# Chunk attention's loop: the order of scores and output product on TensorE, and of maxima and moments on VectorE

## The reference

```python
Q = (x @ Wq + bq).reshape(b, nc, CHUNK, e)      # CHUNK = 64, nc = 16, e = 256
K = (x @ Wk + bk).reshape(b, nc, CHUNK, e)
V = (x @ Wv + bv).reshape(b, nc, CHUNK, e)
local_scores = jnp.einsum('bnqe,bnke->bnqk', Q, K) * scale
local = jnp.einsum('bnqk,bnke->bnqe', jax.nn.softmax(local_scores, axis=-1), V)
cross_scores = jnp.einsum('bnqe,bmke->bnmqk', Q, K) * scale
cross = jnp.einsum('bnmqk,bnke->bnqe', jax.nn.softmax(cross_scores, axis=-1), V)
out = (local + cross).reshape(b, s, e) @ Wo + bo
x = _layernorm(x + out, axis=-1)
```

## Time and profile before

| | |
|---|---|
| median of 3 runs | 1342.64 us (1342.58 to 1343.19) |
| profiled execution | 1344.01 us |
| its span | 1342.3 us |
| TensorE matmul, weight load busy | 1173.1 us, 872.3 us |
| VectorE, ScalarE, GpSimd busy | 846.0, 789.7, 609.5 us |
| mean granted TensorE clock | 0.941 |

### The profile page before, as it was taken

How to read it: one execution, slowest core, us unless ns; L and a number is a source line. 1 busy time by engine, 2 the same in 40 slices (tenths; PEclk the granted TensorE clock), 3 DMA queues, 4 the chain that set the end, 5 groups by cost and what they waited for, 6 DMA issues and landing times. The chain is left out here.

```text
span 1342.3 us, 25832 instructions
## 1 busy us (share of the span) xinstructions
PE 1173.1 (87%) x8247; PEld 872.3 (65%) x8248; DVE 846.0 (63%) x1511; ACT 789.7 (59%) x2121; POOL 609.5 (45%) x641
## 2 busy tenths in 40 slices
PE   7888489667799999999989999999899856999991
PEld 4554267455566777777666677777577645888881
DVE  2588789884245555656345556666577658888883
ACT  2488347424556555665555556655367767777773
POOL 1277537647454521431363322310056614888873
PEclk9999779897699999999999999999999857999996
DMA  9100000000110000000100000100190041333334
GB/s 300 49 1 0 0 1 2 1 16 16 29 36 17 17 17 17 17 17 2 32 16 19 15 18 17 48 1 1 30 347 2 1 167 53 55 55 51 55 51 138
DMA packets 42266, 58.03 MB, mean 43 GB/s; under 512 B 6992, under 2 KB 34768, under 8 KB 42160
## 3 DMA queue, kind: packets, MB, share of 16 engines
q1 hardware_dynamic: 34672, 46.44, 11.5%
q0 software_dynamic: 7488, 10.23, 4.7%
HBM read 32.54 MB, written 13.63 MB: 34 GB/s over the span
## 5 line engine op out<-in xcount | busy, mean ns | idle before, releaser
L2100 DVE TENSOR_REDUCE ga_neg_top<-ps 128x1 f32<-128x128 f32 (+7 forms) x256 | 182.1, 753 | 193.8 <-PE ps L1870 193.5
L1990 ACT COPY ga_e_tr<-ps 128x512 f32<-128x512 f32 (+3 forms) x192 | 92.0, 479 | 173.8 <-PE ps L1879 170.9
L1981 ACT ACTIVATE ga_e<-ps,ga_neg_top 128x128 f32<-128x128 f32 (+7 forms) x256 | 188.2, 743 | 7.5 <-DVE ga_neg_top L2100 6.8
L1879 PE MATMUL ps<-ident,ga_e 128*128 128x128 f32 x1152 | 165.2, 278 | 0.9 <-DVE ga_e_tr L2108 0.8
L1895 PE MATMUL ps<-ga_e_tr,ga_v 128*64 128x256 f32 x1152 | 151.7, 391 | 4.1 <-ACT ga_att L1998 4.1
L1879 PEld LDWEIGHTS ps<-ident,ga_e 128*128 128x128 f32 x1152 | 123.3, 142 | 28.1 <-ACT ga_e L1981 14.7
L2108 DVE COPY ga_e_tr<-ps 128x128 f32<-128x128 f32 (+3 forms) x192 | 106.0, 552 | 35.0 <-PE ps L1879 34.7
L2651 DVE TENSOR_TENSOR ex_w_lo<-ex_gate_up,ex_w_hi 128x1024 fp32r<-128x1024 f32 x78 | 95.5, 1225 | 34.0 <-ACT ex_w_hi L2522 32.0
L2055 POOL TENSOR_TENSOR ga_q_lo<-shared,ga_q_hi 128x1024 fp32r<-128x1024 f32 x15 | 35.5, 2368 | 174.9 <-ACT ga_q_hi L1971 174.9
L1895 PEld LDWEIGHTS ps<-ga_e_tr,ga_v 128*64 128x64 f32 x1152 | 72.5, 136 | 48.9 <-issue 23.3
L489 ACT ACTIVATE ca_e<-ps,ca_neg_top 128x64 f32<-128x64 f32 x256 | 76.7, 358 | 36.2 <-DVE ca_neg_top L528 36.2
(11 more groups left out here) (334 smaller groups left out, 2801.3 us busy)
## 6 DMA issues: line engine op xcount, KB each, us to landing
shared<-shared SPq DMA_DIRECT2D x80, 128.0 KB, 2.4
ex_gate_up<-in_ex_gate_up SPq DMA_DIRECT2D x1, 8192.0 KB, 24.4
ex_down<-in_ex_down SPq DMA_DIRECT2D x1, 4096.0 KB, 35.7
x_tr<-in_x_tr SPq DMA_DIRECT2D x4, 512.0 KB, 6.7
x_nat<-in_x SPq DMA_DIRECT2D x1, 2048.0 KB, 11.6
gated_rows<-shared SPq DMA_DIRECT2D x4, 512.0 KB, 4.5
x_tr<-summed_rows SPq DMA_DIRECT2D x8, 256.0 KB, 4.0
out<-x_tr SPq DMA_DIRECT2D x8, 256.0 KB, 2.1
```

What stands on the lines that cost most here:

```text
L1879: last = nc.tensor.transpose(ps_tr[n % 2][:, (kb - k0) * P:(kb - k0 + 1) * P], e[half][t % 2][:, kb * P:(kb + 1) * P], core.ident[:])
L1981: nc.scalar.activation(e[half][t % 2][:, 0:blocks(t) * P], ps_scores(t, half), ACT.Exp, bias=neg_top[t % 2][:, half:half + 1], accum_out=s ...
L1990: nc.scalar.copy(e_tr[g % 2][:, k0:k1, half, t % 2 * P:(t % 2 + 1) * P], ps_tr[n % 2][:, 0:(k1 - k0) * P].rearrange("p (k t) -> p k t", t= ...
L2100: nc.vector.tensor_reduce(neg_top[t % 2][:, half:half + 1], ps_scores(t, half), AX.X, ALU.max, negate=True).then_inc(top_ready, 1)
```

## The change

On TensorE, the matmul y of u5 with its two waits moves from ahead of the scores of u1 to behind them. On VectorE, z and the moments of u5 (four instructions) move from ahead of the maxima of u1 to behind neg_top. No instruction is added or removed, and no buffer or semaphore changes.

```diff
@@ TensorE, step(...) @@
                         last.then_inc(q_ready, 1)
-                    if u5 is not None:
-                        pe.wait_ge(diag_tr_copied, u5 + 1)
-                        tail.pe_output_free(pe, u5)
-                        nc.tensor.matmul(tail.y, diag_tr[:], vw[:, u5, :], start=True, stop=True).then_inc(tail.y_ready, 1)
                     if u1 is not None:
                         ps = ps_scores[(turn - 1) % 2]
                         pe.wait_ge(q_copied, u1 + 1)
...
                         last.then_inc(s_ready, 1)
+                    if u5 is not None:
+                        pe.wait_ge(diag_tr_copied, u5 + 1)
+                        tail.pe_output_free(pe, u5)
+                        nc.tensor.matmul(tail.y, diag_tr[:], vw[:, u5, :], start=True, stop=True).then_inc(tail.y_ready, 1)
                     if at(u2, TILES - 1):
                         following.pe_context(pe)
@@ VectorE, step(...) @@
                                                 bq[:].unsqueeze(2).to_broadcast([P, KD, P]), ALU.add).then_inc(q_copied, 1)
-                    if u5 is not None:
-                        tail.dve_variance(dve, u5)
                     if u1 is not None:
                         link = Chain(dve, first_step, u1, 1)
                         dve.wait_ge(s_ready, u1 + 1)
...
                         nc.vector.tensor_scalar_mul(neg_top[(turn - 1) % 2][:], top[:], -SCALE).then_inc(top_ready, 1)
                         link.end()
+                    if u5 is not None:
+                        tail.dve_variance(dve, u5)
                     if u4 is not None:
```

## The result

The changed kernel takes 1344.84 us (median of 20 runs, of which one, of 2859.01 us, is left out of the ratio), the kernel before 1342.39 us in as many; the ratio is 1.0016, 95% interval 1.0008 to 1.0023. On 1342.4 us that is +2.1 us, between +1.1 and +3.1. The forecast was +1.0 us; the time lies inside its range, and the sign and the mechanism came as forecast, but the sum was too small by about half. The same kernel measured again gave 1.0010 (1.0000 to 1.0021), +1.3 us, so how far the forecast was too small isn't sharp.

What follows compares the result with a forecast made beforehand. The prediction took two loops of waits, through TensorE and GpSimd, to bound the turn. Entry +0.8, three turns 0 and eight turns +0.2 gave +1.0 us: 1343.6 us by the median, range 1341.0 to 1346.0.

Steps and rivals of the forecast that it cites:

- The bound: Old loop turn of 6.11 us: TensorE's loop through diag_tr and y takes 6.07, GpSimd's through probs and halves 5.95.
- neg_top is held: VectorE's neg_top, due at 2.03 us after xn's start, is held 0.8 us by GpSimd's probs on shared SBUF ports.
- The turn of 6.13: New loop turn, summed along VectorE from xn to the next xn with neg_top held: 6.13 us in place of 6.11.
- The entry, +0.8: Turn from 66.78 us: z0 and its variance come behind neg_top 4, so the block sum is 0.8 us late.
- Eight turns, +0.2: Last eight of the twelve turns: 6.13 us each in place of 6.11, together +0.2 us.
- A shorter wait gives none back: TensorE's granted clock is 1.00 in all these turns, so shortening its wait gains nothing through the clock.
- TensorE runs ahead until it needs only xn and q: In the new turn, y waits for the previous turn's copy, so TensorE's scores are ready when the maxima are due.
- The drain only shifts: After the last scores the old and new orders are the same, so the drain moves in time without changing.
- That neg_top isn't held: Rival: neg_top unheld in its new place, GpSimd's loop of 5.95 us sets the turn; 1341.6 us, chance 0.15.
- That it loses the race between probs and halves: Rival: halves takes the ports before neg_top, which ends 1.34 us later in every turn; 1358 us, chance 0.10.
- That TensorE's wait was the whole bound: Rival: neither hold nor GpSimd's loop counts, VectorE's chain sets turns near 5.6 us; 1338 us, chance 0.05.
- That diag is held too: Rival: VectorE's diag is also held and a second hold follows, 0.3 us a turn; 1347 us, chance 0.05.

Runs made afterwards that it cites:

- VectorE's half alone: Kernel before with only VectorE's part of the edit, y still ahead of the scores on TensorE: 1369.07 us, ratio 1.0191.
- The two runs with probs early: Changed kernel and kernel before, each with maxima in PSUM, recip ahead of the block sum, GpSimd's store behind halves: 1346.84 us (1.0029) and 1347.89 us (1.0040).
- their repair: The two runs with probs early, with probs now also waiting for xn: new order 1339.33 us (0.9990), old order 1340.76 us (0.9989).
- the maxima in PSUM alone: Only the 16 maxima moved from SBUF to PSUM: changed kernel 1343.61 us (1.0011), kernel before 1340.09 us (0.9989).
- TensorE's half alone: Kernel before with only TensorE's part of the edit, y behind the scores, VectorE's order as before: 1343.97 us, ratio 1.0010.
- the first profile: First profile of the changed kernel, which measured 1344.84 us (1.0016); its twelve turns took 75.81 us.
- the second: Second profile, from the unaltered changed kernel measured again: 1343.26 us, ratio 1.0010; its twelve turns took 74.26 us.
- the third profile: Changed kernel unaltered, profiled again for the clock alone; twelve turns 74.24 us, first drain turn 7.74 us.
- the run with the filler: Changed kernel with 16 additional TensorE transposes of a constant into an idle bank in the last turn ahead of the loop: 1343.92 us, ratio 1.0007.
- new order from the loop on: Changed kernel with the old order kept in the written-out turns 0 to 7, the new one only from the loop on: 1342.25 us, ratio 1.0007.

## Why the prediction was right, and where it was too small

**The bound (right).** Two loops of nearly equal length, TensorE's and GpSimd's. VectorE's half alone makes the first longer, and the turns follow it to 7.2 and more. The two runs with probs early and their repair separate them: with GpSimd's loop shortened, most turns of the old order are 5.99 or 6.00, so TensorE's loop bounds it, while the better turns of the new order fall to 5.42 to 5.55, from 5.94 to 6.01 with the maxima in PSUM alone, so GpSimd's loop had bounded it there. TensorE's half alone agrees (6.18), with the reserve made there.

**neg_top is held (right, shown).** It took the 0.86 us of the rows above, and 174 ns in every turn once its input had left SBUF. The turn of 6.13 was measured at 6.08 to 6.11 in five of the eight turns. Three of these have the late, shorter neg_top (0.55 to 0.82 us): since it ends with probs, its start hardly matters.

**The entry, +0.8 (right in size).** 6.62 - 5.89 = 0.73. But it belongs to the filling of the pipeline and is no price of the new order in general, as I had come to think by the time of the experiment. In the trace of after neg_top of the entry ends 0.03 us after halves (72.84 against 72.81) and the block sum starts 1.56 us after z (forecast 1.60).

**Eight turns, +0.2 (too small; the step that was mis-sized).** Measured 49.41 - 48.85 = +0.56. The prediction set its 6.13 against a mean of 6.11 that already holds the old order's turns at the branch (6.19, 6.27), and gave as reason that "extra register time at the loop's branch falls ahead of neg_top and is covered by the hold". In the turn behind the loop's entry it isn't: 6.52 against 6.19, +0.33. VectorE's timeline of after there:

```profile
97.85 0.97 DVE L526 TENSOR_SCALAR ca_neg_top<-ca_top 128x16 f32<-128x16 f32 x1
...
99.77 0.18 DVE L252 BATCH_NORM_AGGREGATE tail_mv<-tail_stats 128x2 f32<-128x6 f32 x1 [0.16 <-DVE tail_stats L250]
100.25 0.15 DVE L253 TENSOR_SCALAR tail_var_eps<-tail_mv 128x1 f32<-128x1 f32 x1 [0.30 <-DVE tail_mv L252]
```

Idle time of 0.30 us stands ahead of eps (aggr to eps 0.48, elsewhere 0.22), thus behind neg_top, where no hold covers it. No run tells what causes it. The other seven turns are together 0.23 longer.

**"A shorter wait gives none back" (a step that was missed).** The prediction used the clock of 1.00 only to rule out a gain. It didn't ask what the clock does where the idle time goes. TensorE's wait for diag_tr, 0.7 us each turn, became a few waits of 1 to 2.7 us for ScalarE and for the drain's diag_tr, and the low clock that came with them was worth +1.6 us in the first profile, 0 in the second, +1.3 in the third. "TensorE runs ahead until it needs only xn and q" was wrong for the same reason: it needs the exponentials too, and waits for them (4.9 us in six turns).

**"The drain only shifts" (wrong in some executions).** 7.74 for 6.43 in the third profile.

Sum, in the loop and the first turn of the drain, against the 79.25 us of before: +2.96, +1.39 and +2.73 in the three profiles. Their mean, +2.4, agrees with the measured +2.1 (1.1 to 3.1). At full clock throughout it is +1.4 (the run with the filler: 74.30 + 6.38 - 79.25), where I had +1.0.

**The rivals.** That neg_top isn't held was refuted by its 0.86 us; its price was wrong too, for with the hold taken away the twelve turns are 0.5 us longer than before, not 1 us shorter. That it loses the race between probs and halves was refuted for neg_top, and yet the race exists: xn lost it when probs was 0.05 us behind. That TensorE's wait was the whole bound is refuted by the changed kernel itself, which has lost that wait and keeps turns of 6.08 to 6.11. That diag is held too was refuted in the loop, where its two instructions take 0.45 us in every turn; once, in the drain (144.54), they take 0.97.

**What stays open.** Why the clock fell in one execution of three with the same idle times, and whether the filler keeps it up. That the new order on TensorE makes the low clock of the drain likelier rests on six profiles of nine against one of four, and in that one it came behind another wait; the counts are small. What makes the turn behind the loop's entry 0.33 us longer is open too. Of the +2.1 us, then, 1.4 is shown turn by turn. The rest may be these dips, but that isn't shown: the interval begins at 1.1, and the second measurement of the same kernel gave 1.3.

## What to carry to other kernels

A wait that stands out in the trace is the only bound only if no other loop of dependences has its length: add up each loop through each engine before moving an instruction, and compare like turns with like, not with a mean that holds the branches. Where VectorE and GpSimd both work on SBUF, ask of a moved instruction what GpSimd will be doing at its new time, however small it is: 16 numbers were held for 0.8 us, and one operand in PSUM freed them. And a wait taken from TensorE may not be gone but gathered elsewhere: in the old order's loop waits of 0.55 to 0.84 us a turn never went with a low clock, while in the changed kernel the one of 2.7 us in the drain did in all three profiles (and didn't in the run with the filler).

## What the runs showed of the hardware that was not expected

- Start order in the trace doesn't say which of the two is held: xn at 92.75 was held for all of probs at 92.80, while xn at 100.17 was ahead of probs at 100.28. In the two runs with probs early xn was held in all four turns in which it led by 0.04 or 0.05 us, and in none with a lead of 0.11 or 0.12. For neg_top the same margin doesn't hold: it took its 0.17 us with a lead of 0.05 us on halves in one trace (third profile) and 0.01 us behind it in another (new order from the loop on).
- A VectorE instruction that waits is let through between two GpSimd instructions 0.08 us apart: neg_top in the changed kernel, in all ten turns in which it was held by probs; halves behind it took 1.26 or 1.27 us, as elsewhere.
- The same code, with idle times ahead of its scores that agree within 0.01 us, ran them at half clock in one execution (5.26 us) and at full clock in another (3.69).
